# Routed experts of a macaron block: gate and up products in plain fp32 instead of a three-part fp32r product

## The reference

```
x = x + 0.5 * ffn(layernorm(x))
x = x + attention(layernorm(x))
x = x + 0.5 * ffn(layernorm(x))

ffn(x):  shared = (silu(x @ Gs) * (x @ Us)) @ Ds            # one shared expert, inner width 256
         p = sigmoid(x @ router_w.T + routing_bias)         # 8 routed experts
         scores, picks = top_2(p); scores /= sum(scores)
         routed = sum over the 2 picks e of score_e * (silu(x @ G_e) * (x @ U_e)) @ D_e
         return shared + routed
```

## Time and profile before

| | us |
|---|---|
| median of three executions | 782.27 |
| the profiled execution, its span | 995.4 |
| in it: dispatch | 223 |
| first slot stage | 260 |
| middle | 240 |
| second slot stage | 244 |
| tail | 28.4 |

### The profile page before, as it was taken

How to read it: one execution, slowest core, us unless ns; L and a number is a source line. 1 busy time by engine, 2 the same in 40 slices (tenths; PEclk the granted TensorE clock), 3 DMA queues, 4 the chain that set the end, 5 groups by cost and what they waited for, 6 DMA issues and landing times.

```text
span 995.4 us, 17656 instructions
## 1 busy us (share of the span) xinstructions
PE 753.1 (76%) x5074; PEld 677.0 (68%) x5074; DVE 571.1 (57%) x1867; ACT 465.6 (47%) x866; POOL 533.5 (54%) x564
## 2 busy tenths in 40 slices
PE   6574748564788887778899999898848787877871
PEld 5563637544787777777766778787647787877871
DVE  7755745344444455555568888776645344545543
ACT  4532333112545554546567766554235455545540
POOL 1656355555555554545507766566635555655552
PEclk9686867766999898989979999988879999998997
DMA  9211111211432433433112211112123423454444
GB/s 295 68 60 43 57 43 36 73 57 65 110 105 81 118 111 108 117 107 113 48 43 65 65 41 36 41 36 73 44 68 94 130 75 116 150 165 136 140 131 137
DMA packets 63448, 89.65 MB, mean 90 GB/s; under 512 B 13178, under 2 KB 43772, under 8 KB 63356
## 3 DMA queue, kind: packets, MB, share of 16 engines
q1 hardware_dynamic: 46460, 53.63, 18.9%
q0 software_dynamic: 16896, 34.90, 10.6%
HBM read 46.36 MB, written 42.12 MB: 89 GB/s over the span
## 4 chain that ended last, share of the span: by engine, by line
PE 50%; issue 16%; DVE 14%; another core or an unknown queue 11%; ACT 6%; DMA 1%; POOL 1%; ACTq 1%; DVEq 0%; POOLq 0%; SPq 0%
PE y_bank L1056 10%; PE g_bank L879 5%; PE u_bank L881 4%; PE y_bank L971 4%; PE g_bank L881 4%; PE u_bank L879 4%; PE g_bank L880 4%; PE u_bank L880 3%; PE tr_bank L901 2%; PE tr_bank L1010 2%; ACT send L701 1%; PE route_bank L1010 1%; DVE xT_lo L1690 1%; ACT silu_g L782 1%
## 5 line engine op out<-in xcount | busy, mean ns | idle before, releaser
L638 POOL DMA_INDIRECT y_rows<-send,y_to x272 | 264.3, 972 | 238.9 <-DVE send L1711 159.9
L626 POOL DMA_INDIRECT x_rows<-send,send_to x256 | 248.9, 972 | 192.9 <-DVE number_weight L1384 87.8
L1699 DVE TENSOR_TENSOR h<-silu_g,u_bank 128x512 f32<-128x512 f32 x136 | 93.3, 686 | 170.3 <-ACT silu_g L782 90.8
L1056 PE MATMUL y_bank<-w_dn,h 128*128 x1088 | 157.5, 291 | 37.8 <-DVE h L1699 29.2
L1056 PEld LDWEIGHTS y_bank<-w_dn,h 128*128 128x128 f32 x1088 | 144.0, 205 | 43.0 <-issue 42.9
L757 ACT ACTIVATE slot_gu<-w_gu 128x1024 fp32r x130 | 137.6, 1058 | 27.1 <-issue 26.4
L879 PE MATMUL g_bank<-xT_hi,slot_gu 128*128 128x256 f32 x260 | 89.6, 345 | 77.7 <-DVE xT_lo L1690 58.5
L879 PEld LDWEIGHTS g_bank<-xT_hi,slot_gu 128*128 128x128 f32 x260 | 53.5, 206 | 87.0 <-DVE xT_lo L1690 65.8
L782 ACT ACTIVATE silu_g<-g_bank 128x512 f32<-128x512 f32 x136 | 79.5, 585 | 35.7 <-remote 16.1
L971 PEld LDWEIGHTS y_bank<-w_dn,h 128*128 128x128 f32 x512 | 72.9, 221 | 30.0 <-issue 27.7
L971 PE MATMUL y_bank<-w_dn,h 128*128 128x128 f32 x512 | 73.5, 305 | 22.8 <-issue 16.8
(11 more groups left out here) (286 smaller groups left out, 1658.8 us busy)
## 6 DMA issues: line engine op xcount, KB each, us to landing
send<-x_rows SPq DMA_DIRECT2D x130, 130.0 KB
y_pair<-y_rows SPq DMA_DIRECT2D x32, 512.0 KB
y_rows<-send,y_to POOLq DMA_INDIRECT x272
x<-x_in SPq DMA_DIRECT2D x16, 256.0 KB, 7.2
x_rows<-send,send_to POOLq DMA_INDIRECT x256
out<-x SPq DMA_DIRECT2D x16, 256.0 KB
w_raw<-w_experts SPq DMA_DIRECT2D x15, 256.0 KB
x_rows<-pad SPq DMA_DIRECT2D x16, 130.0 KB
```

What stands on the lines that cost most here:

```text
L626: pool.indirect_dma_start(x_rows, bass.IndirectOffsetOnAxis(ap=send_to[b % SEND_TO_RING][:, w, k:k + 1], axis=0), send[ring_of(f, t)][:, w ...
L638: pool.indirect_dma_start(y_rows, bass.IndirectOffsetOnAxis(ap=y_to[k][:, j:j + 1], axis=0), y_out[f][k][:, j, :], None).then_inc(y_sent[k ...
L1056: last = pe.matmul(y_bank[par][:, j * P:(j + 1) * P], h[par][0][:, c * ROWS + j * P:c * ROWS + (j + 1) * P], w_dn[:, bass.ds(e[j % len(e)] ...
L1699: dve.tensor_tensor(h[par][0][:], silu_g[par][:], u_bank[par][:], ALU.mult).then_inc(slot_h_done, 1)
```

## The change

Routed experts no longer have split weights. SyncE loads each expert's gate, up and down weights (128x768) straight into `w_all`, all eight right after `x` and the attention weights; the shared expert's come first, in place 0, and it alone is still split (`shared_gu`). Per full slot ScalarE copies the picked expert's 768 columns to one of three buffers `slot_w`, and waits for the down product of three slots before (`slot_y_psum`) where it waited for the up product of two slots before. The rows are copied once, as plain fp32 (`slot_x`), and there is no low part. Gate and up are 4 plain fp32 matmuls of 128x256 per slot. The down product takes its weights from `slot_w` at a fixed address, and the read of the run-time index on TensorE is left in the mixed slots alone.

```diff
@@ -34,6 +34,7@@
 SEND_TO_RING = 4
+W_RING = 3
 TILES = 16
@@ -139,10 +140,11@@
         w_raw = two("w_raw", [P, 2 * INNER])
-        w_gu = sb("w_gu", [P, EXPERTS, 2, 2 * INNER], F32R)
-        w_dn = sb("w_dn", [P, EXPERTS, HALVES, P])
-        slot_gu = two("slot_gu", [P, 2, 2 * INNER], F32R)
-        shared_raw = sb("shared_raw", [P, 2 * INNER])
+        w_all = sb("w_all", [P, EXPERTS, WIDE])
+        shared_raw = w_all[:, 0, 0:2 * INNER]
+        shared_gu = sb("shared_gu", [P, 2, 2 * INNER], F32R)
+        slot_w = ring(W_RING, "slot_w", [P, WIDE])
+        slot_x = two("slot_x", [P, ROWS])
         attn_raw = sb("attn_raw", [P, 4 * P])
@@ -261,7 +263,6@@
         y_in = [y_pair[:, i] for i in range(Y_RING)]
-        mixed_xT = phi_q[0][:, 0:ROWS]
 
@@ -453,8 +451,8@@
 
-        def halves(a):
-            return a.rearrange("p (c n) -> p c n", c=HALVES)
+        def down_of(w, c):
+            return w[:, 2 * INNER + c * P:2 * INNER + (c + 1) * P]
 
@@ -464,25 +462,20@@
             sp.dma_start(bias_b[:], routing_bias.partition_broadcast(P)).then_inc(router_loaded, 16)
-            sp.dma_start(w_raw[0][:], w_experts[0, :, 0:2 * INNER]).then_inc(w_loaded[0], 16)
+            sp.dma_start(w_all[:, 0, :], w_experts[0]).then_inc(shared_loaded, 16)
             for t in range(1, 4):
                 sp.dma_start(x[:, t, :].rearrange("p (b n) -> p b n", b=2), x_view[t]).then_inc(x_some, 16)
-            sp.dma_start(w_dn[:].rearrange("p e c n -> p e (c n)"),
-                         w_experts[:, :, 2 * INNER:].rearrange("e p n -> p e n")).then_inc(down_loaded, 16)
             for t in range(4, tiles):
                 sp.dma_start(x[:, t, :].rearrange("p (b n) -> p b n", b=2), x_view[t]).then_inc(x_rest, 16)
             sp.dma_start(attn_raw[:], w_attn).then_inc(attn_loaded, 16)
-            sp.dma_start(shared_raw[:], w_experts[0, :, 0:2 * INNER]).then_inc(attn_loaded, 16)
             sp.dma_start(bq_col[:], bq).then_inc(attn_loaded, 16)
             sp.dma_start(bv_b[:], bv.partition_broadcast(P)).then_inc(attn_loaded, 16)
             sp.dma_start(bo_rows[:], bo.partition_broadcast(2)).then_inc(attn_loaded, 16)
+            for e in range(1, EXPERTS):
+                sp.dma_start(w_all[:, e, :], w_experts[e]).then_inc(experts_loaded, 16)
             sp.wait_ge(pad_ready, 1)
             sp.dma_start(x_rows[ROUTED * region:].rearrange("(b p j) d -> p b (j d)", p=P, j=JS),
                          nobody_pad.rearrange("p b j d -> p b (j d)")).then_inc(nobody_region, 16)
-            for e in range(1, EXPERTS):
-                wait_count(sp, split_lo, 0 if e == 1 else split_expert(e - 2))
-                sp.dma_start(w_raw[e % 2][:], w_experts[e, :, 0:2 * INNER]).then_inc(w_loaded[e % 2], 16)
 
@@ -550,9 +543,7@@
                 stores = [t for t in range(tiles) if first_add(f, t) + LEAVE - 3 < slots] if f else []
-                if f == 0:
-                    sp.wait_ge(split_lo, split_expert(ROUTED))
-                else:
+                if f == 1:
                     sp.wait_ge(kv_psum, tiles)
@@ -651,9 +642,9@@
         def _(act):
-            def split_high(e):
-                act.wait_ge(w_loaded[e % 2], (e // 2 + 1) * 16)
-                act.activation(w_gu[:, e, 0, :], w_raw[e % 2][:], ACT.Copy).then_inc(split_hi, 1)
+            def split_high():
+                act.wait_ge(shared_loaded, 16)
+                act.activation(shared_gu[:, 0, :], shared_raw, ACT.Copy).then_inc(split_hi, 1)
 
@@ -736,10 +727,8@@
                     for t in ts:
-                        if 1 <= t < EXPERTS:
-                            split_high(t)
                         if t == tiles - 3:
-                            act.wait_ge(attn_loaded, 80)
+                            act.wait_ge(attn_loaded, 64)
                             act.activation(attn_hi[:], attn_raw[:, 0:3 * P], ACT.Copy).then_inc(split_hi, 1)
@@ -753,25 +742,15@@
                 e = act.value_load(w_table[0:1, i:i + 1], min_val=1, max_val=ROUTED)
-                wait_count(act, slot_u_psum, n - 1)
-                act.activation(slot_gu[n % 2][:].rearrange("p a n -> p (a n)"),
-                               w_gu[:, bass.ds(e, 1)].rearrange("p e a n -> p (e a n)").bitcast(F32),
-                               ACT.Copy).then_inc(slot_gu_done, 1)
-            def slot_high(f, s):
+                wait_count(act, slot_y_psum, n - W_RING + 1)
+                act.activation(slot_w[n % W_RING][:], w_all[:, bass.ds(e, 1), :].rearrange("p e n -> p (e n)"),
+                               ACT.Copy).then_inc(slot_w_done, 1)
+            def slot_copy(f, s):
                 n = slot_of(f, s)
                 act.wait_ge(slot_xT_psum, n + 1)
                 wait_count(act, slot_u_psum, n - 1)
-                act.activation(xT_hi[n % 2][:, 0:ROWS], slot_tr[n % 2][:, 0:ROWS], ACT.Copy).then_inc(slot_hi_done, 1)
-            def mixed_copy(f, s):
-                n = slot_of(f, s)
-                act.wait_ge(slot_xT_psum, n + 1)
-                wait_count(act, slot_u_psum, n - 1)
-                if f == 1:
-                    act.wait_ge(att_psum, tiles)
-                act.activation(mixed_xT, slot_tr[n % 2][:, 0:ROWS], ACT.Copy).then_inc(slot_hi_done, 1)
+                act.activation(slot_x[n % 2][:], slot_tr[n % 2][:, 0:ROWS], ACT.Copy).then_inc(slot_x_done, 1)
 
@@ -782,15 +761,14@@
             def slot_stage(f):
-                act.wait_ge(split_lo, split_expert(ROUTED))
+                act.wait_ge(experts_loaded, ROUTED * 16)
                 slot_weights(f, 0)
-                slot_high(f, 0)
+                slot_copy(f, 0)
                 for s in range(slots):
-                    if mixed(s + 1):
-                        mixed_copy(f, s + 1)
-                    elif s + 1 < slots:
-                        slot_high(f, s + 1)
-                        slot_weights(f, s + 1)
+                    if s + 1 < slots:
+                        slot_copy(f, s + 1)
+                        if not mixed(s + 1):
+                            slot_weights(f, s + 1)
                     if f == 0 and s == slots - 1:
@@ -951,7 +929,7@@
                     return
-                w = w_gu[:, 0]
+                w = shared_gu
                 xs = (xT_hi[par][:], xT_lo[par][:])
@@ -968,7 +946,7@@
                     for c in range(HALVES):
-                        last = pe.matmul(shared_bank[:, s], h[t % 2][c][:, s], w_dn[:, 0, c, :], start=(c == 0),
+                        last = pe.matmul(shared_bank[:, s], h[t % 2][c][:, s], down_of(w_all[:, 0], c), start=(c == 0),
                                          stop=(c == HALVES - 1))
@@ -1004,8 +982,7@@
                 pe.wait_ge(rows_loaded[n % ROW_RING], rows_count(n))
-                wait_count(pe, slot_hi_done, n - 1)
-                wait_count(pe, slot_lo_done, full_before(n - 1) if n > 1 else 0)
+                wait_count(pe, slot_x_done, n - 1)
                 for j in range(JS):
@@ -1013,17 +990,16@@
                 par = n % 2
-                pe.wait_ge(slot_lo_done, full_before(n + 1))
-                pe.wait_ge(slot_gu_done, full_before(n + 1))
+                pe.wait_ge(slot_x_done, n + 1)
+                pe.wait_ge(slot_w_done, full_before(n + 1))
                 wait_count(pe, slot_h_done, n - 1)
                 if s == 0:
                     pe.wait_ge(h_done, 2 * (f + 1) * tiles - 1)
-                w = slot_gu[par]
-                xs = (xT_hi[par][:, 0:ROWS], xT_lo[par][:, 0:ROWS])
+                w = slot_w[n % W_RING]
                 for bank_, base, signal in ((g_bank[par], 0, slot_g_psum), (u_bank[par], INNER, slot_u_psum)):
                     for c in range(HALVES):
                         i = slice(base + c * P, base + (c + 1) * P)
-                        last = three(bank_[:, c * ROWS:(c + 1) * ROWS], (w[:, 0, i], w[:, 1, i]), xs)
+                        last = pe.matmul(bank_[:, c * ROWS:(c + 1) * ROWS], w[:, i], slot_x[par][:], start=True, stop=True)
                     last.then_inc(signal, 1)
@@ -1039,14 +1015,16@@
                             last = pe.matmul(bank_[:, k:k + P], mixed_w[q % 2][j][:, base + c * P:base + (c + 1) * P],
-                                             mixed_xT[:, j * P:(j + 1) * P], start=True, stop=True)
+                                             slot_x[par][:, j * P:(j + 1) * P], start=True, stop=True)
                     last.then_inc(signal, 1)
 
             def slot_down(f, s):
                 n = slot_of(f, s)
                 par = n % 2
-                picked = half_entries(s) if mixed(n) else (entry(s),)
-                e = [pe.value_load(w_table[0:1, i:i + 1], min_val=1, max_val=ROUTED) for i in picked]
+                w = [slot_w[n % W_RING]] * JS
+                if mixed(n):
+                    picked = [pe.value_load(w_table[0:1, i:i + 1], min_val=1, max_val=ROUTED) for i in half_entries(s)]
+                    w = [w_all[:, bass.ds(e, 1), :].rearrange("p e n -> p (e n)") for e in picked]
```

(44 more changed lines are left out.)

## The result

The changed kernel takes 808.38 us (median of 4, 804.78 to 810.73), the kernel before 781.12 in the same comparison: a ratio of 1.0344, 95% interval 1.0311 to 1.0378, or 24 to 30 us more. A second comparison gave 806.56 against 783.06, 1.0305 (1.0267 to 1.0342). The forecast was slower, 816 us, range 781 to 830.

What follows compares the result with a forecast made beforehand. The prediction took the slots as bound by TensorE and GpSimd, 2.54 us each. Product +39, dispatch -3 and slack -2 summed to +34 us on the median of 782, so 816 us, range 781 to 830.

Steps and rivals of the forecast that it cites:

- The bound: Both slot stages: TensorE and GpSimd hold nearly all timed slots at 2.54 us each, with little slack.
- The sum of floors: Whole kernel: dispatch 187, middle 218 and tail 28 make 433 us, leaving 349 of the median for 136 slots.
- the surplus: Profiled slots: waits of 1.1 to 1.3 us per slot, said to belong mostly to the profiled execution.
- The product, +39: Gate and up of 130 full slots: TensorE's period becomes 2.84 us against 2.54, 0.30 more each, +39 us.
- this is on the path: Full slots: the longer product counts in full because TensorE, which pays, has no gap.
- The clock: TensorE in the slot stages: 18% of slots at the lower clock would make the product's price 52 us, the upper bound.
- The rest of a slot, 0: Full slots: no low part, a 0.84 us weight copy and a new wait, all covered by TensorE's 2.84 us; 0.
- the third rival: Gate and up: weight loads bound the product, TensorE's slot falls to 2.04 us, GpSimd stays at 2.54; 779 us, chance 0.03.
- Dispatch, -3: Dispatch: eight splits leave ScalarE and VectorE, mostly covered by GpSimd's scatters; -3 us, bounds 0 and -10.5.
- Slack, -2: Slots: the small remainder over the floor, 349 against 345 us, hides some of the longer product; -2 us.
- The first: Slots: something else already makes them take 2.84 us or more, hiding the longer product; 782 us, chance 0.12.
- The second: Slots: the chain transposes, row copy, low part, gate is the bound, so the change is faster; 746 us, chance 0.09.

Runs made afterwards that it cites:

- f3_three_rest: Changed kernel with gate and up again 12 fp32r matmuls, of the single copy of rows and weights; 778.59 us, ratio 0.995 to the kernel before.
- f2_plain_only: Kernel before with only gate and up of full slots made 4 plain fp32 matmuls, low parts made but unused; 813.51 us, ratio 1.0387.
- f1_after: Changed kernel, unchanged, run again where the kernel before takes 783.06 us; 806.56 us.
- g3_before_one_scatter: Kernel before with one of each slot's two result scatters left out and results loaded from the input, on the 1006 us chip; 872.47 us.
- g4_after_one_scatter: Changed kernel with one of each slot's two result scatters left out and results loaded from the input, on the 1006 us chip; 906.72 us.
- g1_before: Kernel before, unchanged, profiled again on the 1006 us chip; 1011.0 us.

## Why the prediction was right, and where its sizes were off

**The bound.** Slots at TensorE's and GpSimd's floors was right where the comparison was made: with three products most slots there are 2.54 us apart, in the changed kernel 2.84 in both stages. The sum of floors that left 349 us for 136 slots found this from a profile whose slots took 3.6 to 3.8. That it fitted so well was luck in part: in f3_three_rest TensorE leaves the dispatch at 164 us and not at 187, and the two slot stages take 370 and not 349. The two errors cancel, because the slots begin before the dispatch's scatters have ended. Its reading of the surplus was wrong: not the profiled execution but the chip makes the waits.

**The product, +39.** The price per slot was right to the hundredth: 0.22 + 1.73 + 0.89, as worked out from another line's shape. Its total is 28.0 us (all else of the change kept) or 30.5 (all else of before kept). The term that was too large is 130 x 0.30, by the step "this is on the path" for the first stage: I saw GpSimd's 2.54 as a floor per slot, and not that GpSimd comes out of the dispatch with TensorE nine slots ahead of it and, with three products, stays the bound for the whole stage. That stage pays 11.1 us of its 19.5, the second 17.4. The clock, which made the upper end of the range, added nothing: the slot stages were granted 0.96 and 1.00 after, and 0.95 and 1.00 with three products.

**The rest of a slot, 0.** The 0.84 us of the weight copy, the missing wait and the unchanged silu came as said. The Trainium skill's price of a weight load (*TensorE: Matmul & The Clock Gate*, LDWEIGHTS), taken as what bounds the product, would have taken time off a slot. The trace disagrees: the plain records of 128x256 are 0.217 us apart with their load records of 0.19 beside them, and the third rival is out.

**Dispatch, -3.** Zero: GpSimd's last scatter there starts at 197.4 with and without the splits.

**Slack, -2, and the rest of the change.** All else is worth 4.5 us with three products (ratio 0.9917 to 0.9982), and 813.51 - 806.56 = 7.0 with the plain one. That is near the 5 forecast by luck: the dispatch, which was to give 3 of them, gave nothing. In the profiles f2_plain_only and f1_after, 7.1 us apart, 4.2 lie in the middle, which the change hardly touches and which differs by 3.6 us between two profiles of the changed kernel itself (221.4 and 217.8). What it comes from stays open.

**The rivals.** The first, that something else than TensorE holds the slots, is true of the first stage with three products, and worth 8 of the 39 us. The second, the chain from the transposes through ScalarE and VectorE to gate, could only hold on the other chips. There the plain product alone, with all steps of that chain kept, already gains 1.6%, so even there it isn't the shorter chain alone. Why a product with more TensorE time in fewer instructions helps on a chip whose slots wait now and then is not settled.

## What to carry to other kernels

Price a change of shape from the distance of record starts of that very shape elsewhere in the trace, and then ask of each stage which engine enters it with a backlog: a longer step on a second engine is free until the backlog is gone. Before a profile with unexplained waits is believed, add up the floors of all stages and hold them against the timed median; if they nearly fill it, the waits are not in the timed runs. And look at a step that has nothing to wait for, such as a register check: here it told the two kinds of chip apart.

## What the runs showed of the hardware

On two chips a step of SyncE's queue that takes 18 ns in the median lasts up to 0.7 us, and the same kernel takes 27 to 28% longer (993 and 1006 us against 783); where the kernel before takes 781 to 783 the step never passes 33 ns. The waits of the slots go with how many scatters a slot has: with one per slot instead of two the slots of such a chip ran at the 2.52 us floor for long stretches, and 136 scatters fewer saved 133 us. At 783 two scatters per slot cause nothing of the kind. That fewer scatters take away most of the slots' waits is shown, on one chip; the step itself is still held, up to 0.44 us in g3_before_one_scatter and 0.70 in g4_after_one_scatter. What in the chip makes it is not shown, nor what makes its dispatch 60 us longer.

An indirect DMA of 128 rows keeps GpSimd 0.97 us and, where nothing holds it, follows the last one after 0.30, so 1.27 from start to start; this is the same at 783 (f3_three_rest) and at 1006 (g1_before).
